# Output projection of a decoder layer's attention in seven block products instead of eight tiles

## The reference

```python
qkv = jax.nn.silu(hidden_states @ qkv_w.T)          # hidden_states: layernorm(x)
scores = jnp.einsum('bhnd,bhmd->bhnm', cq, ck) * diag_decay
attn = ...                                          # scores @ v, causal with decay, 64 tokens
xf = xf * jax.lax.rsqrt(jnp.mean(xf * xf, axis=-1, keepdims=True) + EPS)
normed = norm_w * xf.astype(attn.dtype)
gate = jax.nn.sigmoid(hidden_states @ gate_w.T)
return gate * normed @ out_w.T                      # the output projection, 4096 -> 512
```

## Time and profile before

| | us |
|---|---|
| median of 3 runs (2106.32 to 2108.52) | 2108.07 |
| profiled execution, device time | 2110.23 |
| its span, first to last instruction | 2108.4 |
| mean granted TensorE clock | 0.998 of full speed |
| PE busy | 2066.0 |
| DVE busy | 1397.6 |
| ACT busy | 1127.1 |
| POOL busy | 759.3 |

### The profile page before, as it was taken

How to read it: one execution, slowest core, us unless ns; L and a number is a source line. 1 busy time by engine, 2 the same in 40 slices (tenths; PEclk the granted TensorE clock), 3 DMA queues, 4 the chain that set the end, 5 groups by cost and what they waited for, 6 DMA issues and landing times.

```text
span 2108.4 us, 42509 instructions
## 1 busy us (share of the span) xinstructions
PE 2066.0 (98%) x16208; PEld 1695.7 (80%) x16208; DVE 1397.6 (66%) x1993; ACT 1127.1 (53%) x1928; POOL 759.3 (36%) x882
## 2 busy tenths in 40 slices
PE   5999999999999999999999999999999999999998
PEld 5788888888888888878888888888888888666665
DVE  6566666575666666766666665656666656788885
ACT  4545555454545554555554555545455554666664
POOL 6333435252434343543443342525243433211110
PEclk9999999999999999999999999999999999999999
DMA  3111211111112011111111111111110201311110
GB/s 119 56 62 42 62 41 51 51 51 45 57 35 67 30 62 41 47 38 51 53 42 62 41 52 50 51 51 51 40 62 30 72 30 57 131 42 50 46 36 21
DMA packets 40502, 109.49 MB, mean 52 GB/s; under 512 B 4960, under 2 KB 9568, under 8 KB 40288
## 3 DMA queue, kind: packets, MB, share of 16 engines
q1 hardware_dynamic: 40128, 107.25, 16.0%
q10 hardware_dynamic: 288, 1.05, 0.1%
...
## 4 chain that ended last, share of the span: by engine, by line
PE 95%; DVE 3%; ACT 1%; POOL 0%; issue 0%; DMA 0%; SPq 0%; POOLq 0%; DVEq 0%
PE bank L1059 15%; PE bank L1064 14%; PE bank L1062 14%; PE bank L1116 5%; PE bank L1117 5%; PE bank L1118 5%; PE bank L1079 5%; PE bank L1084 5%; PE bank L1082 5%; PE bank L1106 4%; PE bank L1094 3%; PE bank L1452 3%; PE bank L1465 3%; PE bank L212 2%; PE bank L1491 1%; PE bank L1474 1%
## 5 line engine op out<-in xcount | busy, mean ns | idle before, releaser
L521 POOL TENSOR_TENSOR raw<-raw 128x256 f32<-128x256 f32 x128 | 126.7, 990 | 598.0 <-DMA raw<-w_pairs 598.0
L1059 PE MATMUL bank<-x_hi,w_hi_c 128*128 128x512 f32 x672 | 267.5, 398 | 1.9 <-DVE v L841 1.5
L1064 PE MATMUL bank<-x_hi,w_lo_c 128*128 128x512 f32 x672 | 262.5, 391 | 0.0
L1062 PE MATMUL bank<-x_lo,w_hi_c 128*128 128x512 f32 x672 | 262.5, 391 | 0.0
L1116 PE MATMUL bank<-wo_hi,y_hi 128*128 128x512 f32 x512 | 202.0, 395 | 3.0 <-DVE x_lo L915 1.7
L1117 PE MATMUL bank<-wo_lo,y_hi 128*128 128x512 f32 x512 | 199.7, 390 | 0.0
L1118 PE MATMUL bank<-wo_hi,y_lo 128*128 128x512 f32 x512 | 199.4, 389 | 0.0
L552 POOL TENSOR_TENSOR sq_acc<-sq_acc,sq 128x512 f32<-128x512 f32 x124 | 161.0, 1299 | 92.3 <-ACT sq L715 83.2
L841 DVE TENSOR_TENSOR qk<-bank,qk 128x512 f32<-128x512 f32 x192 | 127.1, 689 | 85.3 <-ACT qk L686 42.7
L1059 PE MATMUL bank<-x_hi,w_hi_a 128*128 128x512 f32 x448 | 176.0, 393 | 0.0
L1064 PE MATMUL bank<-x_hi,w_lo_a 128*128 128x512 f32 x448 | 174.5, 390 | 0.0
(11 more groups left out here) (168 smaller groups left out, 5452.2 us busy)
## 6 DMA issues: line engine op xcount, KB each, us to landing
...
```

The lines of the kernel that those rows point to most:

```text
L521: nc.gpsimd.tensor_tensor(raw[:, S1], raw[:, S3], raw[:, A22], ALU.add).then_inc(done, 1)
L1059: nc.tensor.matmul(bank[:, to], w_hi[w][:, a, s], x_hi[:, b, c], start=part in ("first", "only") and c == 0, stop=False, skip_group_check= ...
L1062: nc.tensor.matmul(bank[:, to], w_hi[w][:, a, s], x_lo[:, b, c], start=False, stop=False, skip_group_check=True)
L1064: i = nc.tensor.matmul(bank[:, to], w_lo[w][:, a, s], x_hi[:, b, c], start=False, stop=part in ("last", "only") and c == 1, skip_group_che ...
```

## The change

The output projection becomes a block product of the same form. The gated rows of a half-group are four blocks Y[h, b] (head h, token half b), the weights four blocks of head and column half. Seven products (`OUTS`) take the place of eight tiles; each is 128-row stationary operands of y against 256 columns of wo, for 512 tokens: 12 matmuls of 256 columns.

- Weights: DRAM layout in blocks, `scale_out` scales raw1 in place on ACT, `mix_out` makes S1 to S4 on POOL, `cut_out` cuts 1792 columns instead of 1024, on ACT and DVE, in two parts.
- Rows: `gated` now writes to `gate` in SBUF instead of PSUM; `y_sum` makes the four differences there on POOL, in place; `y_high` and `y_low` cut one block for each product (two buffers in turn).
- Results: `add_out` adds each product's two halves of tokens, 14 additions per half-group; some products accumulate in PSUM on an earlier product's result, after `add_out` has read that (`IN_BANKS_OF`).
- `sq` has one buffer instead of two, so `square` of b=1 waits until POOL has added b=0, and moves into the first gap of the next call.
- Order: PE's list is now, with o0 to o6 and p0 to p6 as products: VA, p0 p1, VB with p2 inside, p3, QK0 with p4 inside, p5, scores(0,0), QK1 with p6 inside, scores(0,1), G01, weigh(0), QK2, o0 o1, scores(1,0), QK3 with o2 and o3 inside, o4, scores(1,1), o5, G23 with o6 inside, weigh(1).
- Small tensors of the cross attention move to memory of the first stage; their constants load later.

The core of the diff:

```diff
+        OUTS = ((A11, (0, 0), 0, (0, 0), True), (A12, (1, 0), 5, (0, 0), True), (S1, (0, 0), 5, (1, 1), True),
+                (S4, (1, 1), 5, (0, 1), False), (S2, (1, 1), 0, (0, 1), False), (S3, (0, 1), 0, (1, 1), False),
+                (A22, (1, 0), 0, (1, 0), False))
+        IN_BANKS_OF = {2: 1, 3: 2, 4: 0, 5: 4, 6: 5}
...
-        sq = sb(own, "sq", [P, 2, HG, BT])
+        sq = sb(own, "sq", [P, HG, BT])
...
+            def mix_out(half, d, s):
+                pool.wait_ge(wo_scaled, count(half, d, 4, 2 * s + 2))
+                mix(raw1, mixed_o, count(half, d, 8, 4 * s))
+
+            def y_sum(half, d, s, nth):
+
+                b11, b12, b21, b22 = (gate[:, h, b] for h in range(2) for b in range(2))
...
+                to, left, right = ((b11, b12, b11), (b12, b22, b12), (b22, b22, b11), (b21, b21, b22))[nth]
+                nc.gpsimd.tensor_tensor(to, left, right, ALU.subtract).then_inc(y_summed, 1)
...
+                last_block(half, d, QK2)
+                y_sum(half, d, 0, 0)
                 mix0(half, d, 4)
...
+                for nth in range(1, 4):
+                    y_sum(half, d, 0, nth)
...
+                mix_out(half, d, 1)
                 squares(half, d, 1)
+                y_sum(half, d, 1, 0)
+                y_sum(half, d, 1, 1)
...
             def square(half, d, s, b):
...
+                else:
+                    act.wait_ge(y_made, count(half, d, 8, 4 * s + 4))
+                if b or s or before(half, d):
+                    act.wait_ge(sq_added, count(half, d, 8, 4 * s + 2 * b))
...
             def weighted(half, d, s):
                 square(half, d, s, 0)
-                y_high(half, d, s, 0)
-                square(half, d, s, 1)
+                for n in range(2):
+                    y_high(half, d, s, n)
...
+                def in_va():
+                    if previous:
+                        square(*previous, 1, 1)
+                    if at(d, 0):
+                        turned_hi(half, WITH_VALUES[0])
+                    else:
+                        cut_qk0(half, d, 0)
...
+                project(half, d, QK1, lambda: scale_out(half, d, 0), lambda: cut_out(half, d, 0, 0),
+                        lambda: cut_out(half, d, 0, 1))
...
+                project(half, d, QK2, lambda: square(half, d, 0, 1))
...
+                weighted(half, d, 1)
...
+                if following:
+                    for part in range(2):
+                        cut_out(half, d, 1, part)
...
-            def project(half, d, call, between=None, last_gap=None):
+            def project(half, d, call, between=None, last_gap=None, first_gap=None, late_gap=None):
...
                 silu(half, d, call, 0, 1, THIRD, 3)
                 if last_gap:
                     last_gap()
                 silu(half, d, call, 1, 0, CHAIN, 4)
...
+            def add_out(half, d, s, n):
+
+                for k in range(2):
+                    dve.wait_ge(out_mm, count(half, d, 28, 14 * s + 2 * n + k + 1))
...
+                def in_vb():
+                    added(2)
+                    rows_low(4)
...
+                def late_in_qk3():
+                    add_out(half, d, 0, 3)
+                    y_low(half, d, 0, 5)
...
+                project(half, d, VB, last_gap=in_vb)
...
+                project(half, d, QK0, in_qk0, lambda: rows_low(6))
...
+                project(half, d, QK1, lambda: added(6), lambda: cut_out(half, d, 0, 0))
+                cut_out(half, d, 0, 1)
...
-                project(half, d, QK2, lambda: cut_a(half, d, 2, 0))
+                project(half, d, QK2)
...
                 add_out(half, d, 0, 0)
+                cut_a(half, d, 2, 0)
                 cut_a(half, d, 2, 1)
...
+                project(half, d, QK3, in_qk3, late_in_qk3)
...
+            def project_out(half, d, s, n):
+                w, _, first, _, fresh = OUTS[n]
...
+                pe.wait_ge(y_ready, count(half, d, 14, 7 * s + n + 1))
+                for k in range(2):
+                    if n >= 2:
+                        pe.wait_ge(out_added, count(half, d, 28, 14 * s + 2 * IN_BANKS_OF[n] + k + 1))
+                    for i in range(2):
+                        r = slice((2 * k + i) * P, (2 * k + i + 1) * P)
+                        dst = bank[:, first + k, i * 2 * P:(i + 1) * 2 * P]
...
-                project(half, d, QK1, 0)
-                if previous:
-                    rest_out(*previous, 1, (6, 7))
+                project(half, d, QK1, 0, previous and {2: (*previous, 1, 6)})
                 pe.wait_ge(scores_ready, count(half, d, 4, 1))
                 make_scores(half, d, 0, 1)
```

452 lines of the change are left out of this document (263 added, 189 removed).

## The result

The changed kernel took **2387.35 us** in the median of 4 runs (2376.77 to 2390.20), beside 2107.20 us for the kernel before on the same chip (2105.96 to 2108.52). The ratio is 1.1316, with a 95% interval of 1.1297 to 1.1336: 13% slower. The forecast was 2249 us with a range up to 2300. The sign was right and the loss twice as large as forecast (280 us instead of 142). The profiled execution took 2388.78 us, its span is 2386.9, its mean granted clock 0.977.

The account below looks back on a forecast made before the run. PE, busy 98% of the span, was taken as the bound. 2110.2 us profiled + 168 of waits - 24 of gain - 2.5 of a removed wait made 2251.7; less 2.1 for the runs' median, 2249 us, range 2180 to 2300.

Parts of the forecast that it names:

- E: The slot in which PE could go on after the seventh product of a call; waits are counted from it.
- The gain of 24 us: Output projection on PE: 84 matmuls of 256 columns instead of 48 of 512 per half-group, 24 us less.
- Terms 1 to 4: DVE work before a call's last multiplication makes PE wait before scores(0,1), QK0, scores(1,1), scores(0,0): 41.6, 30, 32, 12 us.
- term 1: QK1 to scores(0,1): DVE's cut_out before the last multiplication, no cover behind it; a wait of 2.7, 41.6 us in all.
- Term 5: VA's third and fifth products wait for ACT's two snapshots, made late by work in front; 1.95 a pass, 29 us.
- Term 6: QK2's fifth product waits for the second snapshot, behind gated b=1 and two squares; 0.6 a pass, 10 us.
- Rival C: POOL becomes late by colliding with DVE, delaying QK3's first snapshot and one more place; about 2285 us, chance 20%.
- Term 7: Before QK3: both parts of cut_a come after the last multiplication and two adds; 0.8 a pass, 13 us.
- QK3 inside: QK3's first snapshot, behind POOL's mix0(4) and ACT's cut_g23, ends 0.3 us before its slot; no cost.
- The turn and the ends: The turn of the halves and the tail are moved, not lengthened: within 5 us either way.
- Rival B: Half of the waits: one wait is the next one's cover and small terms vanish; 2170 us, chance 16%.
- Rivals A and D: A: hand-overs hold, matmul count decides, 2084 us, chance 4%. D: gain and waits cancel within 0.2%, chance 1%.

Follow-up runs that it names:

- the count alone: Kernel before, with the output projection as 7 tiles of 12 matmuls of 256 columns instead of 8 of 6 of 512, other engines unchanged: 2096.99 us.
- the last run: Changed kernel's work reordered on ACT, DVE, POOL and PE; against the run before it, POOL multiplies QK3's last block before mixing raw0: 2247.73 us.

## Why the prediction was wrong in size

The way and the place of nearly every wait were right; steps of the sum failed. By the prediction's own steps, with means over the twelve loop passes (the waits are taken from E, so 0.16 us is added to each idle time):

- **The gain of 24 us** (0.121 us per matmul): right. PE's busy time fell by 24.7 us with the count alone; half of it did not become time there.
- **Terms 1 to 4** (scores(0,1) 2.7, VB 2.0, scores(1,1) 2.0, scores(0,0) 0.8): right; 2.9, 2.1, 2.0 and 0.9 us. Each was taken away by moving just the work that was named. In two loop passes of twelve term 1 was 3.3 us, where the cut in front met POOL's multiplication.
- **Term 5** (VA, 1.95): 2.9 us. **Term 6** (QK2, 0.6): 1.6 us. Here the price failed: the two y_low before gated b=1 were put at 0.6 us each, and took 2.3 together beside POOL's additions of squares. Without these additions the two waits were 1.0 and 1.1 us shorter. Rival C had seen such a collision in the earlier trace rows, on the mixes only, where it is POOL that pays.
- **Term 7** (QK3's weights, 0.8): 1.5 us; cut_a took 2.69 us for both parts instead of 2.05, beside POOL's y_sum and mix0(4). That this made the wait longer is argued; no run took it away by itself.
- **QK3 inside** ("ends 0.3 us before its slot", no cost in the forecast, 1.7 us in rival C): 1.46 us of idle time in two waits, 1.8 from the slots. This is the wait put at nothing. Rival C had the place right and half of the mechanism: the third product waited behind POOL's mix0(4), the fifth behind DVE's two cuts for G23, 3.6 us beside y_sum. With the margin named as 0.3 us and a collision of 1 us seen in the earlier trace rows, nothing spoke for the margin.
- **Restarts**: 0.1 us of slower first matmul at each of 8 waits, 0.8 us a pass, not counted at all.
- **The clock**: no term at all. The trace of before (0.998) showed no fall in a loop pass, and the kernel before had no waits behind which it could fall. It cost 1.9 us in the mean of the loop passes (126.2 against 124.3 in the two at full clock).

The forecast's terms make a loop pass of 119.2 us; the mean was 126.2, 7.0 more. The differences above sum to 0.2 + 0.1 + 0.0 + 0.1 + 1.0 + 1.0 + 0.7 + 1.8 + 0.8 + 1.9 = 7.6 us.

**The turn and the ends** were put within 5 us either way, and this step failed too, by 54 us. Of the 138 us between forecast and result 84 lie in the twelve loop passes, 12 in the first pass, 21 in the two passes around the turn of the halves, 3 in the last one and 18 behind the last weigh(1). In the first pass QK0's start waits 3.76 us (1.50 before) and scores(0,1) 3.49 us (1.46 before). At the turn PE waits 5.0 us for POOL before scores(1,1) of the last pass of the first half. In the tail two waits for additions, 3.44 and 2.51 us, and one of 3.7 us for a load of the cross attention's inputs are new. No run tried any of these; their causes stay open.

**Rival B** thought that one wait covers the next. With the gated operations first, waits of 2.3 us closed in VA and QK2 came back in part as one larger wait in QK3, and idle time fell by 1.1 us a pass. That is not because POOL and DVE are full there, though they are busy for 22.6 and 20.5 of 25 us in the changed kernel (489 to 514 us): the last run has the same work, and its waits in QK3 and around scores(1,1) sum to 2.8 us instead of 4.6. So order made them, not the amount of work. **Rivals A and D** had no part.

What stays open is why waits of the same length lower the clock in some passes and not in others.
